# Value rows in two half products: 256 columns instead of 512 per matmul in an AdaLN attention block with a ternary FFN

## The chip, the cores and the metric

One core of a Trainium2 chip runs the whole kernel. The metric is the device time of one execution in microseconds, the median of several runs. Before the change the median of 3 runs is 315.8 us (315.19 to 317.01).

## What is computed

The input `x` has 32 sequences of 32 tokens with 256 channels, 1024 token rows in all, and one condition vector of 256 for each sequence. All arithmetic is float32 in the reference.

```
ada = cond @ ada_w + ada_b                      # shift, scale, gate, twice
x1  = layernorm(x) * (1 + scale1) + shift1
q, k, v = split(x1 @ qkv_w + qkv_b)             # 16 heads of 128: 3 x 2048 columns
p   = softmax(q k^T / sqrt(128))                # 32 x 32 in each sequence and head
x   = x + gate1 * ((p v) @ out_w + out_b)
x2  = layernorm(x) * (1 + scale2) + shift2
y   = x + gate2 * (gelu(x2 @ ffn_w1 + ffn_b1) @ ffn_w2 + ffn_b2)
z   = ternary_linear(silu(ternary_linear(y, w1, g1)) * ternary_linear(y, w2, g2), w3, g3)
out = x_in + z
```

The change touches only how the columns of `v` are made.

## The kernel before, in words

The 1024 tokens are worked in four quarters of 256 tokens (two tiles of 128), and the 16 heads in four groups of 4 heads. One quarter with one group is a unit; there are 16 units, `u` = 0 to 15. The first eight units take the head groups 0 and 1, the last eight take groups 2 and 3 and have the FFN stages of earlier quarters between their parts. The order of every engine's instructions is written out by hand, and engines are kept in step by semaphores alone.

float32 products are made in three passes. Each operand is split into a high part of type float32r and a low part, the remainder, and `three_pass` (L572 to L584) adds high x high, high x low and low x high into one PSUM tile, each pass over both halves (k = 0, 1) of the 256 channels. That is 6 matmuls into one destination, and each has a weight load (LDWEIGHTS) of 128 x 128 of its own. With `late` a wait stands ahead of the last third of them.

In a unit TensorE makes:

- `qk_unit` (L586), once for each of 4 heads: 12 matmuls with 256 moving columns, 6 into the left half of `proj_bank[h % 2]` (the queries, transposed) and 6 into the right half (the keys). The weights are the projection matrix and the moving operand is `x1`. ScalarE reads both halves out (`keep_qk`, L1817).
- `v_unit` (L629), once for each of 2 token tiles: the value rows. Here the `x1` tile is the weight and 512 columns of the value matrix (4 heads x 128) are the moving operand: 6 matmuls into the whole of `proj_bank[t]`, 128 x 512, which is one PSUM bank. VectorE adds the bias row and writes `v_sb` (`keep_v`, L1288), in one instruction for each tile.
- `score` (L640), 32 products of 32 columns, which the trace records as 64; `attend` (L652) of the unit before; and `out_proj` (L683) of the unit before, 24 or 48 matmuls with 256 moving columns.

In the first eight units the order is, from u = 2: heads 0, 1, 2, `attend(u - 1)`, head 3, `v_unit` twice, `score(u)`, `out_proj(u - 1)` twice. In the last eight, even units have `attend` ahead of heads 2 and 3 and then the value rows; odd units have all heads, then `attend`, and then the value rows directly. `tern_total` (L741), one small product for each of three ternary weights, stands between the value rows and the scores of units 2, 4 and 5.

`v_unit(u, 0)` waits for the high part of the group's value weights (`vw_hi`) once, and for their low part (`vw_lo`, made by GpSimd in `low_v`, L2173) as its `late` wait. That matters where a group comes for the first time: units 0, 1, 8 and 9. Each `v_unit` also waits until ScalarE has read the bank that it writes. `projected` counts one for each head and one for each value tile.

Of the kernel before, what the change touches and what calls it, by code (L numbers as in the profile page):

```python
# [67 lines left out]
def adaln_bitffn(nc, x, cond, ada_w, ada_b, qkv_w, qkv_b, out_w, out_b, ffn_w1, ffn_b1, ffn_w2, ffn_b2,  # L68
# [4 lines left out]
    KD = D // P  # L73
# [5 lines left out]
    GC = HG * DH  # L79
# [20 lines left out]
    def group(u):  # L100
        return 2 * (u // HALF) + u % 2

    def quarter(u):
        return u % HALF // 2
# [16 lines left out]
    with ExitStack() as ctx:  # L121
# [3 lines left out]
        def sem(name):  # L125
            return ctx.enter_context(nc.semaphore(name))
# [8 lines left out]
        x1_hi = sb("x1_hi", [P, NQ, KD, QT], F32R)  # L135
        x1_lo = sb("x1_lo", [P, NQ, KD, QT], F32R)
# [8 lines left out]
        SLOT = HALVES * CH  # L145
        WO = SLOT + VW
        w_hi = [sb(f"w_hi{s}", [P, WO], F32R) for s in range(2)]
        w_lo = [sb(f"w_lo{s}", [P, WO], F32R) for s in range(2)]
# [112 lines left out]
        proj_bank, att_bank, wide_bank = [[pair[:, i, :] for i in range(2)] for pair in (proj_banks, att_banks, wide_banks)]  # L261
# [67 lines left out]
        vw_lo = sem("vw_lo")  # L329
# [14 lines left out]
        projected = sem("projected")  # L344
# [226 lines left out]
        def _(pe):  # L571
            def three_pass(dst, pairs, start=True, stop=True, late=None, each=None):  # L572
                hi = [(a, c) for a, b, c, d in pairs]
                left_lo = [(b, c) for a, b, c, d in pairs]
                right_lo = [(a, d) for a, b, c, d in pairs]
                seq = hi + (left_lo + right_lo if late is not None and late[0] == "rhs" else right_lo + left_lo)
                for i, (l, r) in enumerate(seq):
                    if each is not None and i < len(pairs) and i % 2 == 0:
                        pe.wait_ge(each[0], each[1] + i // 2 + 1)
                    if late is not None and i == 2 * len(pairs):  # L580
                        for made, n in late[1:]:
                            pe.wait_ge(made, n)
                    mm = pe.matmul(dst, l, r, start=start and i == 0, stop=stop and i == len(seq) - 1)  # L583
                return mm  # L584
# [44 lines left out]
            def v_unit(u, t):  # L629
                g, Q = group(u), quarter(u)  # L630
                if t == 0:
                    pe.wait_ge(vw_hi, g + 1)
                pe.wait_ge(qk_kept, 2 * HG * u + 2 * HG - 2 + 2 * t)
                tok = slice(t * P, (t + 1) * P)
                cols = [slice(SLOT + k * GC, SLOT + (k + 1) * GC) for k in range(KD)]
                three_pass(proj_bank[t][:, :],
                           [(x1_hi[:, Q, k, tok], x1_lo[:, Q, k, tok], w_hi[g % 2][:, cols[k]], w_lo[g % 2][:, cols[k]])
                            for k in range(KD)], late=("rhs", (vw_lo, g + 1)) if t == 0 else None).then_inc(projected, 1)

            def score(u):  # L640
                pe.wait_ge(qk_kept, 2 * HG * (u + 1))
# [292 lines left out]
            for k in range(KD):  # L934
                mm = pe.transpose(proj_bank[0][:, k * NB:(k + 1) * NB], cond_rows[:, k * P:(k + 1) * P], ident[0:NB, 0:NB])
# [13 lines left out]
            for u in range(HALF):  # L949
# [14 lines left out]
                if u > 1:  # L964
                    attend(u - 1)
                qk_unit(u, HG - 1)
                v_unit(u, 0)
                v_unit(u, 1)
                if u in (2, 4, 5):
                    tern_total((2, 4, 5).index(u))  # L970
# [15 lines left out]
            for q in range(NQ):  # L986
# [5 lines left out]
                qk_unit(u, 2)  # L992
                qk_unit(u, 3)
                v_unit(u, 0)
                v_unit(u, 1)
                score(u)
# [1362 lines left out]
```

## Time and profile before

| | |
|---|---|
| median of 3 runs | 315.8 us (315.19 to 317.01) |
| profiled execution | 315.93 us |
| span of its instructions | 314.1 us |
| TensorE busy (matmul) | 306.4 us, 98% |
| weight loads busy | 272.0 us, 87% |
| VectorE busy | 223.5 us, 71% |
| ScalarE busy | 186.0 us, 59% |
| GpSimd busy | 127.9 us, 41% |
| TensorE share of the chain that ended last | 91% |

The profile is of one execution. Busy is the time in which at least one instruction of the engine was under way; matmuls overlap one another, so what a matmul costs is read from the distance between the starts of neighbours and not from its duration. The chain of waits is the work that ended last, followed backwards from the end.

### The profile page before, as it was taken

How to read it: one execution, taken by the hardware profiler on the slowest of the kernel's cores; microseconds unless marked ns; L12 is line 12 of the kernel's file. 1: busy time of each engine (PE TensorE's matmuls, PEld its weight loads, DVE VectorE, ACT ScalarE, POOL GpSimd, SP SyncE). 2: the span in 40 equal slices, each digit the busy share in tenths (PEclk: the TensorE clock that was granted, in tenths of full speed). 3: DMA queues.
4: the chain of work that ended last, by engine and by line, in shares of the span. 5: the costliest groups of instructions: out<-in, count | busy, mean ns of one | idle time of the engine just before them, and what ended most of it. 6: DMA issues, size and time to landing. Idle time of an engine off the chain costs nothing.

```text
span 314.1 us, 9832 instructions
## 1 busy us (share of the span) xinstructions
PE 306.4 (98%) x4177; PEld 272.0 (87%) x4177; DVE 223.5 (71%) x448; ACT 186.0 (59%) x358; POOL 127.9 (41%) x109
## 2 busy tenths in 40 slices
PE   8999999999999999999999999999999999999986
PEld 6887989899898989989898998789997889998665
DVE  3676789857795994634578057879277888995996
ACT  2765474645534664466345936587555677377793
POOL 2276406200930992766120621247330255216590
PEclk9999999999999999999999999999999999999999
DMA  7798954500043536210020010200110200200011
GB/s 226 261 256 250 272 161 188 167 4 2 2 111 94 160 117 233 69 35 4 1 70 2 2 35 3 68 4 0 34 34 2 69 4 2 69 0 2 0 35 67
DMA packets 21170, 24.48 MB, mean 78 GB/s; under 512 B 2020, under 2 KB 18696, under 8 KB 21128
## 3 DMA queue, kind: packets, MB, share of 16 engines
q1 hardware_dynamic: 20752, 23.57, 24.5%
q8 instruction: 33, 0.54, 0.8%
q10 hardware_dynamic: 376, 0.30, 0.4%
q14 instruction: 9, 0.07, 0.1%
HBM read 22.74 MB, written 1.11 MB: 76 GB/s over the span
## 4 chain that ended last, share of the span: by engine, by line
PE 91%; DVE 4%; ACT 3%; issue 1%; ACTq 0%; DVEq 0%
PE proj_banks L583 43%; PE out_bank L583 17%; PE wide_banks L583 5%; PE turn_bank L583 4%; PE att_banks L679 4%; PE proj_banks L648 4%; PE wide_banks L879 2%; PE att_banks L583 2%; PE wide_banks L679 2%; PE att_banks L926 2%; ACT work L1955 1%; PE wide_banks L762 1%; PE att_banks L879 1%; PE turn_bank L737 1%; PE proj_banks L616 1%
## 5 line engine op out<-in xcount | busy, mean ns | idle before, releaser
L1821 ACT ACTIVATE q_t<-proj_banks,bias_cols 128x256 f32<-128x256 f32 x64 | 30.4, 475 | 50.2 <-PE proj_banks L583 49.5
L583 PE MATMUL proj_banks<-x_hi,w_hi 128*128 128x256 f32 x252 | 52.5, 290 | 0.0
L583 PE MATMUL proj_banks<-x_hi,w_lo 128*128 128x256 f32 x252 | 49.6, 278 | 0.0
L583 PE MATMUL proj_banks<-x_lo,w_hi 128*128 128x256 f32 x252 | 49.5, 278 | 0.0
L583 PEld LDWEIGHTS proj_banks<-x_hi,w_hi 128*128 128x128 f32 x252 | 38.6, 188 | 3.7 <-issue 1.8
L583 PEld LDWEIGHTS proj_banks<-x_hi,w_lo 128*128 128x128 f32 x252 | 38.2, 188 | 0.0
L583 PEld LDWEIGHTS proj_banks<-x_lo,w_hi 128*128 128x128 f32 x252 | 38.2, 188 | 0.0
L1295 DVE TENSOR_TENSOR v_sb<-proj_banks,bv_row 128x512 f32<-128x512 f32 x32 | 21.9, 685 | 16.8 <-PE proj_banks L583 15.7
L1821 ACT ACTIVATE k_t<-proj_banks,bias_cols 128x256 f32<-128x256 f32 x64 | 30.1, 470 | 0.0
L1826 ACT ACTIVATE scores<-scores 128x256 f32<-128x256 f32 x16 | 6.7, 418 | 31.7 <-DVE scores L1304 31.7
L1327 DVE STREAM_TRANSPOSE att_banks<-att_banks 128x512 f32<-128x512 f32 x16 | 11.6, 726 | 18.6 <-PE wide_banks L679 18.1
L583 PE MATMUL out_bank<-wo_hi,at_hi 128*128 128x256 f32 x128 | 21.9, 293 | 0.0
L2229 POOL TENSOR_TENSOR h_lo<-work,h_hi 128x512 fp32r<-128x512 f32 x10 | 13.3, 1332 | 17.3 <-ACT h_hi L1908 16.9
L583 PE MATMUL proj_banks<-w_hi,x_hi 128*128 128x512 f32 x64 | 20.3, 399 | 0.0
L2170 POOL TENSOR_TENSOR w_lo<-stage,w_hi 128x1024 fp32r<-128x1024 f32 x6 | 14.3, 2399 | 14.7 <-DVE w_hi L1250 13.6
L583 PE MATMUL proj_banks<-w_hi,x_lo 128*128 128x512 f32 x64 | 20.0, 393 | 0.0
L583 PE MATMUL proj_banks<-w_lo,x_hi 128*128 128x512 f32 x64 | 19.8, 391 | 0.0
L583 PE MATMUL out_bank<-wo_lo,at_hi 128*128 128x256 f32 x128 | 19.8, 277 | 0.0
L583 PE MATMUL out_bank<-wo_hi,at_lo 128*128 128x256 f32 x128 | 19.8, 277 | 0.0
L2201 POOL TENSOR_TENSOR xa<-xa,out_b_row 128x512 f32<-128x512 f32 x4 | 6.1, 1528 | 33.0 <-ACT xa L1837 33.0
L583 PEld LDWEIGHTS out_bank<-wo_hi,at_hi 128*128 128x128 f32 x128 | 17.2, 188 | 1.0 <-issue 0.2
L583 PEld LDWEIGHTS out_bank<-wo_lo,at_hi 128*128 128x128 f32 x128 | 17.0, 188 | 0.0
(328 smaller groups left out, 791.6 us busy)
## 6 DMA issues: line engine op xcount, KB each, us to landing
stage<-in_L_cond_qkv_w SPq DMA_DIRECT2D x16, 256.0 KB, 3.4
gate<-gate_rows_scratch SPq DMA_DIRECT2D x48, 64.0 KB, 2.4
stage<-in_L_cond_qkv_w SPq DMA_DIRECT2D x4, 512.0 KB, 5.0
stage<-in_L_cond_out_w SPq DMA_DIRECT2D x16, 128.0 KB, 3.6
work<-in_L_ffn_w SPq DMA_DIRECT2D x2, 1024.0 KB, 5.7
xin<-in_x SPq DMA_DIRECT2D x7, 256.0 KB, 2.9
bv_row<-in_L_cond_qkv_b SPq DMA_DIRECT2D x4, 256.0 KB, 7.0
work<-in_L_cond_ada_w SPq DMA_DIRECT2D x1, 1024.0 KB, 8.6
```

The lines of the kernel that those rows point to most:

```text
L583: mm = pe.matmul(dst, l, r, start=start and i == 0, stop=stop and i == len(seq) - 1)
L648: mm = pe.matmul(packed[j * TB:(j + 1) * TB, cols], q_t[:, h, tok], k_t[:, h, tok], start=True, stop=True)
L679: mm = pe.matmul(dst, probs_t[r, t * HG + h, :], v_sb[r, t, h * P:(h + 1) * P], start=True, stop=True)
L879: mm = pe.matmul(banks[i][:, :], qt_bf[:, b, t, i * KD + k, :], w12t[:, i, k, c * MC:(c + 1) * MC], start=(k == 0), stop=(k == KD - 1))
L926: pe.matmul(att_bank[1][:, 0:n * P].rearrange("p (r c) -> p r c", r=n), filler, filler.unsqueeze(1).broadcast_to([P, n, P]), start=True, s ...
L1295: dve.tensor_tensor(v_sb[:, t, :], proj_bank[t][:, :], bv_row[:, u % 2, :], ALU.add).then_inc(v_kept, 1)
L1327: dve.transpose(att_from(u, p), attended_rows(u, p)).then_inc(at_turned, 1)
L1821: act.activation(dst[:, h, :], proj_bank[h % 2][:, s * QT:(s + 1) * QT], ACT.Identity, bias=bias_cols[:, c:c + 1]).then_inc(qk_kept, 1)
L1826: act.activation(scores[:, :, :], scores[:, :, :], ACT.Exp, scale=SM_SCALE).then_inc(exp_done, 1)
L2170: pool.tensor_tensor(w_lo[g % 2][:, s], stage[:, s], w_hi[g % 2][:, s].bitcast(F32), ALU.subtract).then_inc(qk_lo, 1)
L2201: pool.tensor_tensor(xa[:, :, :], xa[:, :, :], rows, ALU.add).then_inc(acc_biased, 1)
L2229: pool.tensor_tensor(h_lo[:, m, :], hf(2 * j, 2), h_hi[:, m, :].bitcast(F32), ALU.subtract).then_inc(h_lo_made, 1)
```

## The change

In `v_unit` the destination of each token tile is split in two halves of 256 columns. The left half gets its six matmuls (high x high, and the two low passes), and then the right half gets its six. A tile so takes 12 matmuls of 256 columns, with 12 weight loads, where it took 6 of 512 with 6 loads. The `late` wait for the low part of the value weights stands in the left half of tile 0. The count on `projected` is still raised once for each tile, at the last matmul of the right half, so the reader `keep_v` and its waits are as before. Order, buffers and all other stages are unchanged.

```diff
                 tok = slice(t * P, (t + 1) * P)
-                cols = [slice(SLOT + k * GC, SLOT + (k + 1) * GC) for k in range(KD)]
-                three_pass(proj_bank[t][:, :],
-                           [(x1_hi[:, Q, k, tok], x1_lo[:, Q, k, tok], w_hi[g % 2][:, cols[k]], w_lo[g % 2][:, cols[k]])
-                            for k in range(KD)], late=("rhs", (vw_lo, g + 1)) if t == 0 else None).then_inc(projected, 1)
+                for n in range(2):
+                    cols = [slice(SLOT + k * GC + n * GC // 2, SLOT + k * GC + (n + 1) * GC // 2) for k in range(KD)]
+                    mm = three_pass(proj_bank[t][:, n * GC // 2:(n + 1) * GC // 2],
+                                    [(x1_hi[:, Q, k, tok], x1_lo[:, Q, k, tok], w_hi[g % 2][:, cols[k]],
+                                      w_lo[g % 2][:, cols[k]]) for k in range(KD)],
+                                    late=("rhs", (vw_lo, g + 1)) if t == 0 and n == 0 else None)
+                mm.then_inc(projected, 1)
```

## Rows read from the trace of the kernel before

**Rows 1.** The page: busy time and the chain that ended last, by engine.

```profile
PE 306.4 (98%) x4177; PEld 272.0 (87%) x4177; DVE 223.5 (71%) x448; ACT 186.0 (59%) x358; POOL 127.9 (41%) x109
PE 91%; DVE 4%; ACT 3%; issue 1%; ACTq 0%; DVEq 0%
```

**Rows 2.** Groups of TensorE's instructions by shape: busy us, mean ns | idle us before.

```profile
L583 PE MATMUL proj_banks<-x_hi,w_hi 128*128 128x256 f32 x252 | 52.5, 290 | 0.0
L583 PE MATMUL proj_banks<-w_hi,x_hi 128*128 128x512 f32 x64 | 20.3, 399 | 0.0
...
L583 PEld LDWEIGHTS proj_banks<-w_hi,x_hi 128*128 128x128 f32 x64 | 10.8, 188 | 2.1 <-issue 0.8
```

**Rows 3.** Timeline of TensorE, unit 1: start us, us from first start to last end.

```profile
27.34 0.39 PE L583 MATMUL proj_banks<-x_hi,w_lo 128*128 128x256 f32 x2
27.57 0.62 PE L583 MATMUL proj_banks<-w_hi,x_hi 128*128 128x512 f32 x2
...
29.86 0.63 PE L583 MATMUL proj_banks<-w_hi,x_lo 128*128 128x512 f32 x2
30.41 0.76 PE L648 MATMUL proj_banks<-k_t,q_t 128*32 128x32 f32 x64
```

**Rows 4.** Timeline of TensorE, units 6 and 7, around an attention stage.

```profile
105.00 0.39 PE L583 MATMUL proj_banks<-x_hi,w_hi 128*128 128x256 f32 x2
...
108.85 0.39 PE L583 MATMUL proj_banks<-x_hi,w_lo 128*128 128x256 f32 x2
109.17 0.30 PE L679 MATMUL att_banks<-v_sb,probs_t 32*32 32x128 f32 x2
...
110.17 0.50 PE L583 MATMUL proj_banks<-x_hi,w_hi 128*128 128x256 f32 x2
110.51 0.40 PE L583 MATMUL proj_banks<-x_lo,w_hi 128*128 128x256 f32 x2
...
111.69 0.63 PE L583 MATMUL proj_banks<-w_hi,x_hi 128*128 128x512 f32 x2
112.16 0.63 PE L583 MATMUL proj_banks<-w_hi,x_lo 128*128 128x512 f32 x2
...
114.55 0.76 PE L648 MATMUL proj_banks<-k_t,q_t 128*32 128x32 f32 x64
```

**Rows 5.** The chain of waits in order of time: start us, us, what.

```profile
38.15 0.44 PE turn_bank L737 x4
41.17 4.38 PE proj_banks L583 x24
49.30 4.08 PE proj_banks L583 x36
63.80 4.24 PE proj_banks L583 x36
69.04 4.32 PE proj_banks L583 x24
122.32 5.67 PE proj_banks L583 x36
138.07 2.96 PE proj_banks L583 x12
186.29 5.79 PE proj_banks L583 x36
```

**Rows 6.** Timeline of all engines at unit 0's value rows.

```profile
13.52 2.39 POOL L2175 TENSOR_TENSOR w_lo<-stage,w_hi 128x1024 fp32r<-128x1024 f32 x1 [7.73 <-ACT w_hi L1847]
15.66 0.62 PE L583 MATMUL proj_banks<-w_hi,x_hi 128*128 128x512 f32 x2
...
16.35 0.41 PEld L583 LDWEIGHTS proj_banks<-w_lo,x_hi 128*128 128x128 f32 x2
...
16.57 0.62 PE L583 MATMUL proj_banks<-w_lo,x_hi 128*128 128x512 f32 x2
```

**Rows 7.** Timeline of GpSimd: the low value weights of units 1 and 9.

```profile
24.61 2.40 POOL L2175 TENSOR_TENSOR w_lo<-stage,w_hi 128x1024 fp32r<-128x1024 f32 x1 [2.14 <-ACT w_hi L1847]
...
130.01 2.40 POOL L2175 TENSOR_TENSOR w_lo<-stage,w_hi 128x1024 fp32r<-128x1024 f32 x1
```

## The prediction, made before the changed kernel ran

> **What bounds the kernel now.** I read the page first: TensorE is busy for 98% of the span and holds 91% of the chain that ended last, so nearly every nanosecond put on TensorE moves the end [rows 1]. The groups by shape come next, for how many instructions the change touches: 64 matmuls in each of three passes have 512 columns, 192 in all, 12 in each of the 16 units, and TensorE sat idle before none of them [rows 2]. Their mean durations (399 ns against 290 ns for 256 columns) are no price, since neighbours overlap. The price is the distance between starts, so the timeline comes third, and the chain of waits last, for how often each pattern occurs.
>
> **Two paces.** The timeline shows two steady paces for 256 columns. From 105.00 to 108.85 there are 34 steps in 3.85 us, 113.3 ns each [rows 4]; I call that the quick pace. From 110.51 to 111.69 there are 10 steps in 1.18 us, 118 ns each (117.5 before rounding to the row's hundredths), the slow pace [rows 4]. The chain says the same over longer stretches: 36 products in 4.08 us at one place and in 4.24 us at another, 4.4 ns apart for each [rows 5]. A stretch tends to keep the pace it has. The products of 512 columns step by 229 ns: from 27.57 to 29.86 ten steps in 2.29 us [rows 3]. After a slow stretch the first two take 0.47 us (111.69 to 112.16), so 235 ns each, and then they too fall to 229 [rows 4]. So the product of 512 columns pulls TensorE out of the slow pace, and the product of 256 does not.
>
> **The change part by part.**
>
> Removed: 192 matmuls of 512 columns and 192 weight loads. Added: 384 of 256 columns with 384 loads. The moving columns in sum are the same. I price it for each unit, from the first value matmul to the first score matmul.
>
> (a) Units that enter the value rows at the quick pace with a head just before. Before: 30.41 - 27.57 = 2.84 us [rows 3]. After: 23 steps of 113.3 ns are 2.61 us, and the step from the last 256-column product into a group of another shape is 109.17 - 108.85 - 0.113 = 0.21 us, read at the same kind of boundary, into the attention products [rows 4]. Sum 2.81 us, so 0.03 us less. There are 6 such units: the ones that start 12 products before the end of the chain's pieces of 24 in 4.32 us (one) and of 36 in 5.67 to 5.69 us (four, of which one stands), and unit 0, where the first pair of value products takes 0.62 us as in the quick unit [rows 3, 5, 6]. 6 x -0.03 = -0.18 us.
>
> (b) Units that enter at the slow pace. Before: 114.55 - 111.69 = 2.86 us [rows 4]. After, if the pace stays slow for lack of a 512-column product: 23 x 117.5 ns = 2.70 us, and 0.21 us, sum 2.91 us; so 0.05 us more. There are 6: five pieces of 24 in 4.38 us (one stands) and one of 36 in 5.79 us [rows 5]. 6 x 0.05 = +0.30 us.
>
> (c) Four units have the attention products directly ahead of the value rows; the chain shows 12 products in 2.96 us in each (one stands) [rows 5]. Entering from the attention products costs a first step of 0.225 us with 256 columns (the pair takes 0.50 us where later ones take 0.40, and the third starts 0.34 us after the first) [rows 4]. Before, the row of 2.96 us is one step of 0.34, ten of 0.229 and one of 0.32 into the scores. After, quick: 0.225 + 22 x 0.1133 + 0.21 = 2.93, 0.03 less. After, slow: 0.34 for the first two, 21 x 0.1175 and 0.21, sum 3.02, 0.06 more. Nothing in the trace says which, as each occurs about equally often behind the attention products. I take the middle, 4 x 0.015 = +0.06 us, with ends of -0.12 and +0.24 us.
>
> (d) The late wait in units 0, 1, 8 and 9. It now comes after 4 products of 256 columns instead of 4 of 512, so 0.46 us earlier. In unit 0 the weight load behind it was due at 16.35; now it is due at 15.66 + 3 x 0.113 = 16.00. GpSimd's piece ends at 13.52 + 2.39 = 15.91 [rows 6]. That leaves 0.09 us. Behind the wait stand everything that TensorE has left and, through it, `keep_v`. The wait was over by 16.35 at the latest, so the price lies between 0 and 0.35 us; I take 0, since GpSimd's row ends ahead of the new due time. In unit 1 the piece ends at 27.01, ahead of 27.57, and in unit 9 at 132.41, ahead of 138.00 [rows 3, 5, 7].
>
> (e) The readers. `projected` is raised at the end of the last product. Before, a tile's last start is 5 x 229 ns = 1.15 us after its first, and that product lasts 0.39 us; after, 11 x 113.3 = 1.25 us and 0.28 us. Both end at 1.53 us. VectorE and ScalarE get their tiles at the same time to within 0.05 us, and no wait of theirs moves more. The waits for a free bank stand where they stood.
>
> (f) 192 more products and as many loads on TensorE's queue, beside 4177 of each [rows 1]. The scores have 64 products in 0.76 us with their own loads, some 10 ns apart [rows 4], so taking in a pair of instructions does not need 113 ns and I price this at 0. The weight load stays hidden: at the quick pace each product of 256 columns already has a load with it. The nearest sign of a floor is the four transposes of 128 columns in 0.44 us, 109 ns apart with half of the columns [rows 5]; 256 columns stand just above it. If the floor were what showed, every product would go at the slow pace, which is the rival below.
>
> Sum: -0.18 + 0.30 + 0.06 + 0 = about +0.2 us on the profiled execution of 315.93 us, of which 314.1 us is the span and 1.8 us lies around it. The profiled execution is 0.1 us above the median of the runs shown, 315.8 us. I predict 316.0 us: no change that can be measured. I call within 0.5% (1.6 us) the same, which is about what repeated runs can tell, with three runs of before 1.8 us apart.
>
> The trace's step for 512 columns, 229 ns, is more than twice the quick step for 256, 113.3 ns [rows 3, 4]. The Trainium skill, page "TensorE: Matmul & The Clock Gate", section "Back-to-back issue gap", has it the other way round: a warm product costs its columns at 2.4 GHz and about 2.5 ns on top, 262 cycles for 256 columns and 518 for 512. By that an estimate of the sum would be 192 x 2.5 ns = +0.5 us. The trace does not bear out the fixed part for these float32r products.
>
> The same section gives another price, for streams of load and product: about 81 ns at 128 columns and 131 ns at 512. On a straight line between these, two products of 256 would cost some 65 ns more than one of 512, an estimate of +12 us for 192. The trace disagrees on the ground of it: 512 columns take 229 ns here and not 131 [rows 3].
>
> **The rivals.**
>
> Quick throughout: the halves fall to the quick pace by themselves. Then (b) gives 2.81 against 2.86, -0.05 us for 6 units, (a) -0.18 and (c) -0.12: -0.6 us, 315.2 us. For it: several stretches after a switch of shape turn quick after a few steps. Against: five value blocks are entered slowly after ten slow steps that did not turn [rows 4, 5].
>
> Slow throughout: the weight load's floor shows in all value products. Then (a) goes from 2.84 to 2.91, +0.07 for 6 units, (b) +0.30, (c) +0.24: +1.0 us, 316.8 us. Against: with `x1` or the output weights as the moving operand the quick pace is the commoner one.
>
> The slow pace spreads: this one ends on the other side. Today every value block ends at the quick pace, and 512 columns bring that about. If a block that ends slow hands its pace over the scores to the 60 products behind it (24 of the output projection, 36 of the next heads), each stretch costs 60 x 4.4 ns = 0.26 us [rows 5]. With the six slow blocks that is +1.6 us over the sum, 317.6 us, and from six such stretches on it is slower by more than 0.5%. Against: the scores and the attention products change the shape, and behind them a slow stretch is as often followed by a quick one. For it: two paces with a memory are what the trace shows, and nothing in it shows a value block that ended slow. With half of these stretches it is 316.8 us.
>
> The late wait in unit 0 bites: +0.35 us at most, 316.3 us. It decides only together with others.
>
> **How the numbers follow.** My forecast has 0.5, quick throughout 0.15, slow throughout 0.1, the spread 0.15 (a third of it beyond 317.4), and 0.1 is left for what I have not seen, on either side. The same within 0.5% is the forecast, both of the uniform cases and most of the spread: 0.83. Slower 0.11, from the spread and the unseen. Faster 0.06: the unseen, or the quick pace carried into stretches that are slow now. The range goes from 315.0, just under quick throughout, to 317.3, where most of the spread is in.
>
> **What would show it.** The group of 64 with 512 columns becomes groups of 128 with 256, and the value block of a quick unit takes 2.81 us. The units entered slowly take 2.91 us at 117.5 ns for each step; if they show 113.3, the claim that only 512 columns end the slow pace is wrong. An idle piece in unit 0 at 16.0 us would show the late wait. The pieces of 36 and 24 behind the scores show the spread: 4.08 us that become 4.24. A step well above 118 ns in the value block, or a time outside 314.2 to 317.4 us, makes the prediction wrong.

## The result and the profile after

| | before | after |
|---|---|---|
| median | 315.79 us (314.72 to 317.01, 22 runs) | 317.04 us (315.03 to 319.14, 22 runs) |
| profiled execution | 315.93 us | 316.65 us |
| its span | 314.1 us | 314.7 us |

The ratio is 1.0042, with a 95% interval of 1.0027 to 1.0058: some 1.3 us slower. That is a small loss clear of noise, inside what the prediction called the same. A second measurement of the same kernel gave 1.0079 (1.0051 to 1.0106), so the loss itself is known only to about 1 us. In the experiments a few executions, of the kernel before as of the edited ones, have a mean granted clock of 0.995 and take 2 to 4 us longer; they count in the ratios, and without them the mean loss of experiments 2, 3, 4, 6 and 8 is 0.1 to 0.5 us smaller and that of experiment 7 is 0.2 us larger.

The page of the changed kernel, which answers to [rows 1]:

```profile
PE 306.5 (97%) x4369; PEld 282.0 (90%) x4369; DVE 226.2 (72%) x448; ACT 185.5 (59%) x358; POOL 127.8 (41%) x109
PE 88%; DVE 4%; ACT 3%; DMA 2%; issue 1%; SPq 1%; ACTq 0%; DVEq 0%
```

TensorE has 192 products and 192 loads more and is busy as long as before. The weight loads' busy time grew by 10 us beside an engine that stayed busy for as long. The groups by shape answer to [rows 2]: 128 of 256 columns where 64 of 512 stood.

```profile
L583 PE MATMUL proj_banks<-w_hi,x_hi 128*128 128x256 f32 x128 | 25.6, 281 | 0.0
```

Unit 8's value rows, timeline of TensorE, the counterpart of the quick block in [rows 3]. The block starts at 124.59 and the scores at 127.40, 2.81 us, with 22 steps of 113.3 ns up to 127.08:

```profile
124.36 0.39 PE L583 MATMUL proj_banks<-x_hi,w_lo 128*128 128x256 f32 x2
124.59 0.39 PE L583 MATMUL proj_banks<-w_hi,x_hi 128*128 128x256 f32 x2
...
127.08 0.39 PE L583 MATMUL proj_banks<-w_hi,x_lo 128*128 128x256 f32 x2
127.40 0.76 PE L651 MATMUL proj_banks<-k_t,q_t 128*32 128x32 f32 x64
```

Unit 9's value rows, directly behind the attention products. Pairs now start 0.23 to 0.24 us apart, the slow pace of 117.5 ns a product, up to the last one, and the block takes 3.02 us from 137.47 to 140.49:

```profile
137.47 0.50 PE L583 MATMUL proj_banks<-w_hi,x_hi 128*128 128x256 f32 x2
137.81 0.40 PE L583 MATMUL proj_banks<-w_hi,x_lo 128*128 128x256 f32 x2
...
140.17 0.39 PE L583 MATMUL proj_banks<-w_hi,x_lo 128*128 128x256 f32 x2
140.49 0.76 PE L651 MATMUL proj_banks<-k_t,q_t 128*32 128x32 f32 x64
```

The chain of waits, which answers to [rows 5]. The piece at 41.05 is 12 head products and 24 half products, 4.30 us where 4.38 stood; the pieces of 24 in 3.02 us (one stands) are the four blocks behind the attention products, which took 2.96 each before; the pieces of 48 in 5.85 us stand against 5.67 to 5.79:

```profile
41.05 4.30 PE proj_banks L583 x36
109.81 4.43 PE proj_banks L583 x36
121.83 5.64 PE proj_banks L583 x48
137.54 3.02 PE proj_banks L583 x24
148.11 5.85 PE proj_banks L583 x48
```

In steps of the trace, the blocks of the changed kernel against those of before: units 0, 2 to 6 and 8 are shorter by 0.03 to 0.05 us (-0.26 us in sum), units 7 and 9 to 15 longer by 0.06 to 0.08 us (+0.52 us). The largest single difference lies outside the value rows. Behind unit 11's scores there are 144 products of 256 columns that the change does not touch. They took 16.63 us before and 17.16 us after, busy throughout in both, first before and then after:

```profile
168.66:185.29 16.63, 16.63 (x155) 16.49 (x162) 4.52 (x10) 9.66 (x19) 5.16 (x4) 1.00 0.00 1
```

```profile
168.35:185.51 17.16, 17.16 (x155) 17.03 (x161) 4.54 (x10) 9.67 (x19) 5.21 (x4) 1.00 0.00 1
```

The columns are the window, its length and then the busy time of TensorE, the weight loads, VectorE, ScalarE and GpSimd, with the granted clock (1.00 in both, the level of 2.4 GHz), DMA share and GB/s. The same work on a busy engine at the same clock is 0.53 us longer, 3.7 ns for each product: it ran at the slow pace, which no wait in the trace explains.

The opening differs too, and its difference cannot be laid to the edit. In unit 1 the changed kernel's block takes 3.66 us, because VectorE gets its bias row late. Its idle time ahead of the first `v_sb` ends at 29.45, long after the products:

```profile
29.45 0.69 DVE L1298 TENSOR_TENSOR v_sb<-proj_banks,bv_row 128x512 f32<-128x512 f32 x1 [3.12 <-issue]
```

A second profile of the kernel before has the same at 28.99, so this wait belongs to both kernels and can hide what is done to units 0 and 1:

```profile
27.79 1.20 issue
28.99 0.70 DVE v_sb L1295
```

The first profile of before is no exception: its row lands at 29.21 and this `v_sb` starts at 29.29. In 13 of the 14 profiles of this case it starts within 0.1 us of that landing, which, experiment 9 with its long opening left out, comes anywhere from 28.5 to 30.5 us. Unit 2 then starts between 41.90 and 43.62 us. Single profiles differ by more than the loss in their openings alone.

### The profile page after: what moved, and what is told of

It reads as the page before. It is cut to its first block, busy times and chain, and to the rows that moved or that the text cites. A ratio compares the mean times of both kernels' runs of the same rounds, so it can differ in the third digit from the quotient of the medians.

```text
span 314.7 us, 10216 instructions
## 1 busy us (share of the span) xinstructions
PE 306.5 (97%) x4369; PEld 282.0 (90%) x4369; DVE 226.2 (72%) x448; ACT 185.5 (59%) x358; POOL 127.8 (41%) x109
## 4 chain that ended last, share of the span: by engine, by line
PE 88%; DVE 4%; ACT 3%; DMA 2%; issue 1%; SPq 1%; ACTq 0%; DVEq 0%
PE proj_banks L583 43%; PE out_bank L583 17%; PE wide_banks L583 5%; PE turn_bank L583 4%; PE proj_banks L651 4%; PE att_banks L682 4%; DMA stage<-in_L_cond_qkv_w 2%; PE att_banks L583 2%; PE wide_banks L882 2%; PE wide_banks L682 1%; ACT work L1958 1%; PE wide_banks L765 1%; PE att_banks L882 1%; PE wide_banks L916 1%; PE att_banks L916 1%
## 5 line engine op out<-in xcount | busy, mean ns | idle before, releaser
L583 PE MATMUL proj_banks<-w_hi,x_hi 128*128 128x256 f32 x128 | 25.6, 281 | 0.0
L583 PE MATMUL proj_banks<-w_lo,x_hi 128*128 128x256 f32 x128 | 25.3, 279 | 0.0
L583 PE MATMUL proj_banks<-w_hi,x_lo 128*128 128x256 f32 x128 | 25.2, 278 | 0.0
L583 PEld LDWEIGHTS proj_banks<-w_hi,x_hi 128*128 128x128 f32 x128 | 19.4, 188 | 0.8 <-issue 0.8
L583 PEld LDWEIGHTS proj_banks<-w_lo,x_hi 128*128 128x128 f32 x128 | 19.4, 188 | 0.1
L583 PEld LDWEIGHTS proj_banks<-w_hi,x_lo 128*128 128x128 f32 x128 | 19.4, 188 | 0.0
```

## The experiments

The theory tested is the one of the prediction, with its rival in the last part: TensorE runs products of 256 columns at one of two paces, a block of halves keeps the pace that it is entered with, and a slow end is handed on. Against it stood a fixed price for each added product, and the wait for the low value weights in units 0 and 1. Each ratio is against the kernel before on the same chip. Differences of single blocks and stretches are against its first profile, which may come from another chip.

### 1. The changed kernel once more

No edit.

> The changed kernel once more, for a second profile. The pace theory (a product of 512 columns ends the slow pace of 117.5 ns, one of 256 does not, and a block that ends slow hands it on over the scores) expects the same ratio as the first time, 1.003 to 1.006, four value blocks directly behind the attention products at 3.02 us, and at least three of the last five blocks at the slow pace. The rival, that the added time is the early part (the wait for the low value weights and the bias row that lands late in units 0 and 1), expects the loss to come and go with the opening, and the blocks of units 8 to 15 to differ from the first profile. A fixed price for each added product expects +0.07 us in every block, quick or slow.

Measured: 317.62 us, ratio 1.0079 (1.0051 to 1.0106). The four blocks behind the attention products took 3.02 us again, and six of the last seven blocks were slow. The eight blocks of units 0 and 2 to 8 were all quick and 0.03 to 0.04 us shorter than before, and still the kernel is slower. The ratio is above the 1.003 to 1.006 expected, a miss on the high side. The long stretch behind unit 11 was quick this time (its 24 FFN products took 2.72 us, 2.83 in the first profile). The stretch behind unit 15 was slow instead:

```profile
137.11 3.02 PE proj_banks L583 x24
169.50 2.72 PE wide_banks L583 x24
252.33 3.02 PE proj_banks L583 x24
256.05 3.02 PE out_bank L583 x24
```

A slow block so does not decide the next stretch. It can at most shift the odds. A fixed price in every block is refuted: quick blocks are shorter than before.

### 2 and 3. Halves in one token tile alone

```diff
-                for n in range(2):
+                if t == 0:            # experiment 2; t == 1 in experiment 3
+                  for n in range(2):
...
+                else:
+                  mm = three_pass(proj_bank[t][:, :], ...)   # 512 columns
```

> Halves in token tile 0 alone; tile 1, the later one, has its 6 products of 512 columns again. 96 products are added instead of 192. The pace theory expects every block to end at the step of 229 ns, so that nothing is handed on: stretches behind the scores as before, and a time within 0.2% of before (-0.2 to +0.5 us). A fixed price for each added product expects half of the loss, +0.6 us, and the early wait in unit 0 and 1 (still 0.46 us sooner) expects all that it costs to stay.

> Halves in token tile 1 alone; tile 0, the earlier one, has 512 columns and keeps the late wait where it was before. The pace theory expects the 512 columns of tile 0 to bring the quick pace and tile 1 to keep it: every second tile at 113.3 ns a step, blocks 0.015 us shorter than before, and a time of -0.5 to +0.2 us against before. A fixed price expects +0.6 us. The theory of the early wait expects no loss.

Measured: 1.0046 (1.0024 to 1.0069) for tile 0 and 1.0048 (1.0020 to 1.0076) for tile 1. Both are misses of the pace theory, which gave at most +0.5 us for either. With halves in tile 0 the slow pace ended in tile 1 in all six blocks that were slow there, at once or after one step of 235 ns. In unit 11, here, the two steps from 165.72 to 166.19 are 0.46 us before rounding, the quick pace already:

```profile
165.49 0.40 PE L583 MATMUL proj_banks<-w_hi,x_lo 128*128 128x256 f32 x2
165.72 0.62 PE L583 MATMUL proj_banks<-w_hi,x_hi 128*128 128x512 f32 x2
166.19 0.62 PE L583 MATMUL proj_banks<-w_lo,x_hi 128*128 128x512 f32 x2
```

Unit 9 of the same profile is an exception to what the other runs show. Its halves stand directly behind the attention products and yet run at the quick pace, ten steps in 1.13 us from 137.87 to 139.00:

```profile
137.53 0.50 PE L583 MATMUL proj_banks<-w_hi,x_hi 128*128 128x256 f32 x2
137.87 0.39 PE L583 MATMUL proj_banks<-w_hi,x_lo 128*128 128x256 f32 x2
...
139.00 0.62 PE L583 MATMUL proj_banks<-w_hi,x_hi 128*128 128x512 f32 x2
```

With halves in tile 1 the wide products of tile 0 did not secure the quick pace. In five of the 16 units (2, 7, 9, 12 and 14) tile 1 was slow; in unit 9 tile 1 ran at 117.5 ns right behind them (138.74 to 139.92, ten steps in 1.18 us):

```profile
138.29 0.62 PE L583 MATMUL proj_banks<-w_lo,x_hi 128*128 128x512 f32 x2
138.74 0.40 PE L583 MATMUL proj_banks<-w_hi,x_hi 128*128 128x256 f32 x2
...
139.92 0.39 PE L583 MATMUL proj_banks<-w_hi,x_lo 128*128 128x256 f32 x2
```

The blocks of these profiles sum to +0.01 and +0.02 us against before, so the measured +1.5 us lies elsewhere. The fixed price's +0.6 us lies at the lower end of both intervals (0.8 and 0.6 us) and so fits little better.

### 4. Halves only behind the attention products

```diff
+                if u > HALF and u % 2 == 1:     # units 9, 11, 13, 15: halves, else 512 columns
```

> Halves only in the four blocks that stand directly behind the attention products (units 9, 11, 13 and 15). The pace theory expects these four at 3.02 us against 2.96 (+0.25 us in sum), and behind unit 11 the long stretch of 143 products at the slow pace (+0.5 us), so +0.5 to +1.0 us in all from a third of the added products' number. A fixed price expects a quarter of the loss, +0.3 us. The early wait of units 0 and 1 expects none.

Measured: 316.56 us, ratio 1.0047 (1.0024 to 1.0070), as much as the whole change with a quarter of its products. All four blocks took 3.02 us, and the stretches behind units 11 and 15 were slow. The ratio means +1.5 us (0.8 to 2.2): its middle is above the range expected (+0.5 to +1.0 us), and a fixed price (+0.3 us) lies outside the interval.

```profile
137.89 3.02 PE proj_banks L583 x24
170.03 2.83 PE wide_banks L583 x24
253.49 3.02 PE proj_banks L583 x24
257.21 3.02 PE out_bank L583 x24
```

The same profile corrects the prediction in another place: three blocks of 512 columns in it, entered slowly, stayed slow to the end, at 233 ns a step.

### 5. The kernel before once more

> The kernel before, once more, for a second profile of it. The pace theory expects a typical one to show few slow products in units 8 to 15 (about 170 of 680 outside the value rows, where the changed kernels showed 233 to 351), the long stretch behind unit 11 at the quick pace, and the last value block followed by the quick pace. The rival, that the pace of a stretch is drawn anew in every execution whatever stands before it, expects this second profile to show other stretches slow than the first, and as many as the changed kernels.

Measured: one execution of 315.61 us, span 313.8 us. Partly against the theory: 260 products outside the value rows were slow between 120 and 256 us, where the first profile of before had 173 of 682, and the long stretch behind unit 11 was slow (2.83 us for its 24). The pace outside the value rows is a draw for the kernel before as well. The value blocks of units 2 to 9, by contrast, were as long as in the first profile to 1 ns.

### 6. Halves only in units 0 to 7

> Halves only in units 0 to 7, 96 products added. No unit there has its value rows directly behind the attention products. The pace theory expects those blocks mostly quick, 0.03 us less each, units 8 to 15 as before, and a time of -0.3 to +0.3 us against before. A fixed price for each added product, or for a longer program, expects half of the loss or all of it: +0.6 to +1.3 us. The early wait for the low value weights in units 0 and 1 expects +0.2 to +0.4 us.

Measured: ratio 1.0034 (1.0008 to 1.0061). Units 2 to 7 were entered slowly and took 0.06 us more than before (0.08 in unit 4, which was quick before), as (b) of the prediction has it, so that with unit 0 the blocks add 0.33 us against the first profile of before. The expectation that they would be mostly quick was wrong. The measured +1.1 us (0.3 to 1.9) is above the range expected and is for the most part not accounted for by the profile, whose span was 313.8 us. A loss of this size without any of the four blocks behind the attention products speaks against putting the whole loss into those four.

### 7. The complement: 512 columns only behind the attention products

> The complement of halves behind attention alone: halves in 12 blocks, and whole products of 512 columns in units 9, 11, 13 and 15, which stand directly behind the attention products. 144 products are added. The pace theory expects these four at 2.96 us, no slow pace handed on from them, and a time within 0.4 us of before. The rival that any added product costs (7 ns each) expects +1.0 us.

Measured: 316.45 us, ratio 1.0008 (0.9987 to 1.0028). Three quarters of the change, and no loss that can be told from none, as the pace theory has it; the +1.0 us of a fixed price is just outside the interval, which ends at +0.9 us. The interval overlaps that of experiment 6, whose 96 added products are all among these 144, so this run alone does not place the loss. The four blocks were at 2.96 us (2.97 once), although ten of the twelve halved blocks were slow (unit 1 among them, with its stall):

```profile
41.23 4.44 PE proj_banks L583 x36
122.40 5.85 PE proj_banks L583 x48
138.31 2.96 PE proj_banks L583 x12
170.38 2.72 PE wide_banks L583 x24
```

### 8. Pass by pass over both halves

```diff
+                for l, r in ((x1_hi, w_hi), (x1_lo, w_hi), (x1_hi, w_lo)):
+                    for k in range(KD):
+                        for n in range(2):      # left, right, with the same weight tile
...
+                    if t == 0 and i == 8:
+                        pe.wait_ge(vw_lo, g + 1)
```

> All value products in halves as in the changed kernel, in another order: each pass makes the left and the right half one after the other, with the same weight tile in both, and the late wait stands behind 8 half products, 0.9 us after the first, as late as before the change. The pace theory expects the same loss as the changed kernel, +1.0 to +2.0 us, since it is the width that counts. The theory of the early wait in units 0 and 1 expects the time of before. If a second load of the same weight tile came cheaper, blocks would take less than 2.81 us.

Measured: 317.25 us, ratio 1.0044 (1.0016 to 1.0072), the loss of the changed kernel. With the late wait back in its old place nothing is won, and experiments 3 and 4 lost as much with it there, so the early wait is refuted as the cause. (The profiled execution took 318.75 us; its bias row landed at 30.49, and unit 2 began 1.0 us later than in the profile of before.) Blocks at the quick pace took 2.81 us and at the slow pace 2.91: a load of the same weight tile again is as dear as any other.

### 9 and 10. More instructions elsewhere

The time outside the span was 1.80 us (mean, 33 executions) in the kernel before, and 2.21 us (22) and 2.59 us (11) in the changed one; 2.04 us in experiment 8, and 1.81 to 1.89 us in experiments 2, 3, 4, 6, 7 and 12. Only kernels with all 32 tiles halved show it, and not in every execution: single ones of the changed kernel have 1.78 to 3.05 us, and three of twelve in experiment 8 have 2.5 to 2.7 us, the others 1.75 to 2.1.

```diff
+            for n in range(96):                                        # experiment 9
+                pe.matmul(att_bank[1][0:TB, 0:P], ident[0:TB, 0:TB], ident[0:TB, 0:P], start=True, stop=True)
...
+            for n in range(384):                                       # experiment 10
+                sp.wait_ge(out_sent, 16)
```

> The kernel before with 192 more products on TensorE, small ones of 32 rows into a bank that nobody reads then, right at the start (96 calls, each recorded as two products with two loads); the value rows are whole. Its span grows by the products themselves, some 3 to 6 us, which isn't the question. The question is the part of the time that lies outside the span: 1.80 us before, 2.2 and 2.6 us (mean) with 192 added half products, 1.81 to 1.89 with 96. If the number of TensorE's instructions sets that part, it reads 2.2 us or more here. If it hangs on the halves themselves, it stays at 1.80.

> The kernel before with 384 more instructions on SyncE: waits on the output transfers that are already met or met at once, behind its last work but one. If the length of the program as a whole, on any engine, sets the part outside the span, it reads 2.2 us or more; if it is TensorE's own list, it stays at 1.80. The span may grow by what the waits take at the end, up to a few us.

Measured: the times are 357.97 us (ratio 1.1329) and 326.93 us (1.0348), four executions each, far more than expected; the last section comes back to this. Outside the span it was 1.83 us with 192 more products on TensorE (mean of 4), and 1.86 us with 384 more instructions on SyncE (mean of 4, 1.79 to 1.96). TensorE had the changed kernel's count to the instruction:

```profile
PE 346.8 (97%) x4369; PEld 304.8 (86%) x4369; DVE 224.1 (63%) x448; ACT 185.5 (52%) x358; POOL 127.6 (36%) x109
```

So the number of TensorE's instructions does not set this part, and nor does that of SyncE's, as far as four executions each can tell. What does is open.

### 11. Quarters in unit 10

```diff
+                if u == 10:
+                    for n in range(4):          # 128 columns each
```

> The kernel before with the value rows of unit 10 alone in quarters: 48 products of 128 columns in place of 12 of 512. The disputed floor by itself: if a load and product cannot follow one another faster than 109 ns (the transposes' step), the block takes 47 steps of 109 ns and the entry into the scores, 5.3 us, against 2.85 whole. If the price were by columns alone, it would take 2.8 us still.

Measured: one execution, of 317.56 us. The block ran from 150.37 to 155.77, 5.40 us for 48 products, from 150.77 to 155.46 one each 111.7 ns:

```profile
150.77 0.39 PE L583 MATMUL proj_banks<-w_hi,x_lo 128*128 128x128 f32 x2
...
155.46 0.39 PE L583 MATMUL proj_banks<-w_hi,x_lo 128*128 128x128 f32 x2
155.77 0.42 PE L656 MATMUL proj_banks<-k_t,q_t 128*32 128x32 f32 x27
```

Half of the columns save 1.6 ns. So a pair of load and product has a floor here, 111.7 ns at 128 columns, and 256 columns stand just on top of it. Whether the load or something else sets it was not tested. The floor lies below both paces, so it is not what makes the slow pace, as the prediction's second rival had it. Going from halves to quarters costs 2.6 us in this unit.

### 12. Halves only in units 8 to 15

> Halves only in units 8 to 15, 96 products added, four of the eight blocks directly behind the attention products. The pace theory expects these four at 3.02 us (+0.24), the other four between -0.03 and +0.07 each, more slow products outside the value rows in these units than the two profiles of before show (173 and 260), and +0.7 to +1.5 us in all, as with the four blocks alone. A fixed price for each added product expects +0.5 us, and the same as halves in the first eight units.

Measured: 316.44 us, ratio 1.0028 (1.0014 to 1.0043), +0.9 us. The four blocks behind the attention products took 3.02 us, the others -0.03, -0.03, -0.04 and +0.08 us against before; 199 products outside the value rows were slow in these units, between the two profiles of before (173 and 260) and not above both, a miss. Experiment 4, with the four blocks behind the attention products alone, had lost 1.5 us. The +0.5 us of a fixed price is inside this interval (0.4 to 1.4 us), so here it is the blocks, and not the time, that speak against it.

### The profiles together

Between 120 and 256 us some 680 products of 256 columns stand outside the value rows. How many of them ran at the slow pace (steps of 116 to 125 ns) in each profile:

| halves behind the attention products in all | | 512 columns there | |
|---|---|---|---|
| changed, 1st and 2nd profile | 351, 233 | before, 1st and 2nd profile | 173, 260 |
| experiments 4, 8, 12 | 321, 417, 199 | experiments 6, 7 | 148, 202 |
| mean | 304 | mean | 196 |

Of the stretches that follow one of these four blocks, 11 of 20 were slow behind halves, and 3 of 16 behind 512 columns. The difference of 108 slow products is 0.48 us at 4.4 ns each. It is a shift of odds read from nine executions, not a rule for one: of the 126 ways to split these nine numbers into five and four, six give a difference as large. The other profiles, counted the same way to within a few products, agree in part. Experiments 9, 10 and 11, with 512 columns there, have 149, 184 and 196. Experiments 2 and 3, with one half-width tile in each of the four blocks, have 256 and 341, although only one of their eight stretches behind those blocks was slow. So slow products also gather where no slow block stands before them.

A firmer reading is the time from unit 8's first value product to unit 15's first score product. It is 130.5 to 131.0 us in the six profiles with 512 columns behind the attention products (before twice, experiments 6, 7, 9 and 10; mean 130.73) and 130.9 to 131.8 us in the five with halves there (the changed kernel twice, experiments 4, 8 and 12; mean 131.35); experiments 2 and 3 have 131.1 and 131.4. Between the means lie 0.62 us, of which the four blocks are 0.24. Outside these units the pace of units 2 to 7 did not follow the edit: units 3, 5 and 6 were slow in all four profiles of chip 15 (experiments 5 to 8), quick in all four of chip 2 (experiments 1 to 4), and either on chip 1.

Over the same nine profiles, 30 halved blocks were entered slowly from a head's products and all 30 stayed slow; 27 of 30 entered quickly stayed quick (the other three are unit 1, behind a stall); all 20 behind the attention products were slow. (Experiment 2, not among the nine, has the one such tile that was quick.) Of the blocks with 512 columns, 15 of 18 entered slowly ended at 229 ns, and all 46 others did. Experiments 9 to 11 make it 24 of 33. One step tells the two kinds apart in advance: from the last head product to the first of the block it was 118 or 119 ns in those 24 and 120 ns in the nine that stayed slow.

## Why the prediction was right, and where it was not

It forecast 316.0 us with a range of 315.0 to 317.3 and a change within 0.5%. The range held, and the change is within 0.5%, but measured it is +0.4% and the forecast was +0.06%: it was right by its bounds and too low in its middle. That the range held is in part luck, since two things that made most of the loss, the blocks of (c) together with the slow stretches and a time outside the span, were priced near nothing in the sum.

**(a) Quick blocks, 2.81 us:** measured 2.81 us, to the row. Halves at the quick pace are cheaper than 512 columns, and the Trainium skill's fixed 2.5 ns for each warm product (page "TensorE: Matmul & The Clock Gate", section "Back-to-back issue gap"), which it gives for an isolated product, did not show here: 24 products took less than 12 of twice the width.

**(b) Slow blocks, 2.91 us:** measured 2.91 and 2.92 us in units 7 and 10 of the changed kernel and in units 3, 6 and 7 of experiment 6, and never did a halved block leave the slow pace. The count was a draw, or hung on the chip: the changed kernel's first profile had units 2, 3, 5 and 6 entered quickly, experiments 6 and 7, both on one chip, had them slow. The sentence that 512 columns pull TensorE out of the slow pace was too strong: 24 of 33.

**(c) Blocks behind the attention products: the step that failed.** It weighed quick against slow as equally likely and took +0.015 us each. Whole halved blocks there were slow each time, 20 of 20, at +0.06 us: +0.24 us in place of +0.06. (Of the four half-width tiles there in experiment 2 one was quick, so it is not a law.) Its two ends were right; the choice between them was made from head products behind the attention products, which the trace shows at either pace.

**(d) The late wait:** in unit 1 it did hold TensorE for about 0.17 us, as that block began 0.95 us earlier than in the profile read, and the bias row's arrival covered it. Moved back in experiment 8, it gave nothing.

**(e) and (f)** held in the trace: unit 1 apart, VectorE's two `v_sb` start within 0.07 us of where they did, counted from the block's first product, and the added instructions opened no gap. Outside the span the sum had a constant, 1.8 us, and there the changed kernel has 0.4 to 0.8 us more. No rival had that.

**The spread** was given 0.15. It is what happened in part: 0.5 us on average and 0.53 us in one stretch of the first profile. With the slow blocks and the part outside the span, (c) +0.24, the spread +0.48 and +0.41 outside make 1.1 us of the 1.3 measured. That account is put together from averages over different executions. With the 0.62 us read from units 8 to 15 in place of the first two terms it is 1.0 us. Experiments 4 and 7 fit it, one with most of the loss from four blocks and the other with little without them. Experiments 2, 3, 4 and 6 lost more than their profiles show, and 12 lost less than 4. So the part in units 8 to 15 is shown and the rest is not. The loss does not grow with the number of added products (48, 96, 144 and 192 gave 1.5, 0.9 to 1.5, 0.3 and 1.3 to 2.5 us). An edit that adds nothing was not timed, so a loss of some tenths that comes with any edit is not excluded. Why the pace has two levels was not found.

## What to carry to other kernels

Price a matmul by the distance between starts in a steady stretch, and look for more than one steady value. Here a float32r product with its load took 111.7 ns at 128 columns, and 256 columns at 113.3 ns stand just above that: splitting down to there won 0.03 us in a quick block, and splitting further nearly doubled the time. That the slow pace stays because no margin is left is a reading of this, and not shown. A narrower product might pay if a reader could begin at the half; here the count was raised for the whole tile, and no run tried the other. When a kernel's unchanged stretches move by 0.5 us between two executions, take several profiles of both kernels before blaming a stage.

## What the runs showed that was not expected

- Two paces of the same instruction, 113.3 and 117.5 ns, at an unchanged granted clock of 1.00, each held for up to 144 products (the prediction had the paces, but not that an untouched stretch changes its pace between executions of one kernel).
- In experiment 9, 192 products on one and the same 32 x 32 tile took 41.16 us, 214 ns each, where the attention products, which go round the tiles, start 7 to 17 ns apart. Each load took 173 ns from just behind the start of the product before, and the next product started some 40 ns after the load's end. The products also shared one destination, so whether the tile or the destination held them apart is open. The expectation had 3 to 6 us.

```profile
3.47 41.16 PE L934 MATMUL att_banks<-ident 32*32 32x128 f32 x192
```

- In experiment 10, 384 waits that were met at the kernel's end took the span from 313.7 us (median of before on that chip) to 325.4 us, some 30 ns each by division; the trace does not show them one by one. The expectation had a few us.
